# Row sums as a 65th column of the attention-value matmuls, and the copy of v in two halves

## The reference, cut to what matters

```python
xn = _layernorm(x, axis=-1)
s = _L0_attn_ref(xn, Wq, Wk, Wv, Wo)
g = _silu(_L0_ffn_ref(xn, rhs))
x = x + s * g
...
q = (x @ Wq.T).reshape(B, S, NHEAD, HEAD_DIM).transpose(0, 2, 1, 3)
k = (x @ Wk.T).reshape(B, S, NHEAD, HEAD_DIM).transpose(0, 2, 1, 3)
v = (x @ Wv.T).reshape(B, S, NHEAD, HEAD_DIM).transpose(0, 2, 1, 3)
...
# a query attends to the 128 keys up to and with its own
scores = jnp.einsum('bhcid,bhcjd->bhcij', qc, k2) / jnp.sqrt(D)
attn = jax.nn.softmax(jnp.where(valid, scores, -inf), axis=-1)
out = jnp.einsum('bhcij,bhcjd->bhcid', attn, v2)
return out.reshape(B, S, E) @ Wo.T
```

## Time and profile before

| | |
|---|---|
| median of 2 runs | 941.93 us (941.15 to 942.71) |
| the profiled execution | 942.05 us |
| its span, slowest core (core 7) | 940.5 us |
| spans of all cores | 928.4 to 940.5 us |
| mean granted TensorE clock of the cores | 0.967 to 0.975 |
| PE, DVE, ACT busy | 76%, 56%, 45% of the span |

### The profile page before, as it was taken

The page is one execution under the profiler, slowest core; times in us unless marked ns, Lnnn a source line. Parts: engine busy times, 40 slices in busy tenths (PEclk is TensorE's granted clock), DMA queues, the critical chain, the costliest instruction groups (busy, mean ns, idle before and its releaser), DMA issues.

```text
span 940.5 us, 15213 instructions; the slowest of 8 cores (928.4 to 940.5 us)
## 1 busy us (share of the span) xinstructions
PE 718.1 (76%) x5649; PEld 374.2 (40%) x5649; DVE 522.1 (56%) x984; ACT 424.5 (45%) x385; POOL 17.2 (2%) x36
## 2 busy tenths in 40 slices
PE   0000378888888888988888888888898899888874
PEld 0000234444444444444444444444444444444442
DVE  3235325666665566665665665655666665565632
ACT  0000145555555545555555555555554554554540
POOL 7000000000000000000000000000000000000000
PEclk9999999999999999999999999999999999999995
DMA  8991732444445434444343544444333444433421
GB/s 159 192 172 45 156 68 56 102 101 101 91 101 102 83 87 101 102 102 95 93 91 71 102 102 101 99 94 101 90 93 88 102 101 101 97 94 70 72 52 56
DMA packets 193048, 91.40 MB, mean 97 GB/s; under 512 B 179272, under 2 KB 179656, under 8 KB 192976
## 3 DMA queue, kind: packets, MB, share of 16 engines
q1 hardware_dynamic: 188368, 82.04, 38.7%
q0 software_dynamic: 4608, 8.39, 5.9%
HBM read 37.98 MB, written 16.78 MB: 58 GB/s over the span
## 4 chain that ended last, share of the span: by engine, by line
PE 52%; DMA 17%; ACT 15%; DVE 7%; issue 6%; SPq 2%; ACTq 0%; DVEq 0%
PE p_proj L461 37%; PE p_av L565 12%; DMA bfp<-bfp 11%; DMA scr<-rhst 6%; ACT bfp L402 4%; ACT bfp L428 3%; ACT bfp L406 3%; ACT bfp L387 3%; PE p_sc L478 1%; PE p_sc L483 1%; SPq L160 1%; DVE sm L292 1%; DVE scr L351 1%; ACT bfp L400 1%; DVE bfp L324 1%
## 5 line engine op out<-in xcount | busy, mean ns | idle before, releaser
L461 PE MATMUL p_proj<-wbf,bfp 128*128 128x512 bf16 x1536 | 367.2, 395 | 58.9 <-ACT bfp L406 31.6
L461 PEld LDWEIGHTS p_proj<-wbf,bfp 128*128 128x128 bf16 x1536 | 149.1, 101 | 241.0 <-issue 94.0
L461 PE MATMUL p_proj<-qrhs,bfp 128*128 128x512 bf16 x512 | 115.6, 379 | 43.6 <-ACT bfp L428 43.6
L565 PE MATMUL p_av<-wbf,bfp 128*128 128x512 bf16 x512 | 118.3, 385 | 4.9 <-DMA bfp<-bfp 4.9
L433 ACT ACTIVATE scr<-scr 128x1024 f32<-128x1024 f32 x32 | 33.8, 1056 | 173.9 <-DVE scr L342 173.9
L461 PEld LDWEIGHTS p_proj<-qrhs,bfp 128*128 128x128 bf16 x512 | 47.8, 97 | 111.5 <-issue 58.5
L381 ACT ACTIVATE bfp<-p_sc 128x2048 bf16<-128x2048 f32 x32 | 60.1, 1877 | 58.5 <-PE p_sc L483 56.3
L351 DVE TENSOR_TENSOR scr<-p_av,scr 128x1024 f32<-128x1024 f32 x32 | 39.2, 1225 | 76.8 <-PE p_av L565 76.8
L415 ACT ACTIVATE q32t<-scr,sm 128x1024 int32<-128x1024 f32 x32 | 36.8, 1148 | 93.3 <-DVE bfp L302 92.5
L565 PEld LDWEIGHTS p_av<-wbf,bfp 128*128 128x128 bf16 x512 | 50.7, 99 | 67.2 <-issue 8.5
L324 DVE TENSOR_TENSOR bfp<-bfp,mstd_s 128x2048 bf16<-128x2048 bf16 x60 | 71.0, 1222 | 4.7 <-ACT bfp L394 4.4
(11 more groups left out here) (58 smaller groups left out, 885.0 us busy)
## 6 DMA issues: line engine op xcount, KB each, us to landing
scr<-x SPq DMA_DIRECT2D x32, 512.0 KB, 4.8
y<-scr SPq DMA_DIRECT2D x32, 512.0 KB, 2.9
scr<-rhst SPq DMA_DIRECT2D x8, 512.0 KB
bfp<-bfp SPq DMA_TRANSPOSE x160, 3.2
wbf<-wqt POOLq DMA_DIRECT2D x8, 256.0 KB, 15.3
wbf<-wkt POOLq DMA_DIRECT2D x8, 256.0 KB, 25.7
wbf<-wvt POOLq DMA_DIRECT2D x8, 256.0 KB, 36.0
wbf<-wot POOLq DMA_DIRECT2D x8, 256.0 KB, 46.5
```

What stands on the lines that cost most here:

```text
L461: mms.append(lambda kc=kc, half=half: tensor.matmul(p_proj[:, half * 512:(half + 1) * 512], lhs_t[:, lhs_base + kc * 128:lhs_base + kc * 1 ...
L565: mms.append(lambda kc=kc, half=half, c=c: tensor.matmul(p_av[:, half * 512:(half + 1) * 512], bfp2[:, AOT[c % 2] + kc * 128:AOT[c % 2] + ...
```

## The change

The values of each head are stored with a stride of 65 instead of 64 columns; the 65th column of each head in both halves of `VS` is set to one once, at the start. A head's attention-value matmul reads 65 columns, so that the row sum comes out beside the 64 values, and the two matmuls against `onesc` are gone. The result goes to `p_sc`, 128 columns to a head, and no longer to `p_av`; VectorE's reciprocal and product read it there. The wait for `comb` of the previous chunk, which kept `AVS` from overwriting `p_av`, now stands ahead of the output projection.

ScalarE copies v out of `p_proj` in two instructions of 512 columns, with tags `vev0` and `vev`. The ffn projection waits for `vev0` ahead of its first matmul, which writes the first half, and for `vev` ahead of its second, which writes the other.

```diff
--- before.py
+++ after.py
@@ -33,11 +33,11 @@
 QB = [4096, 5120]
 QLT = [6144, 7168]
 KT = [8192, 9216]
-VS = [10240, 11264]
-QTF = 12288
-QTM = [13312, 15360]
-QROW, KROW = 17408, 18432
-BFP_COLS = 19456
+VS = [10240, 11280]
+QTF = 12352
+QTM = [13376, 15424]
+QROW, KROW = 17472, 18496
+BFP_COLS = 19520
 
 ERAW = 0
 EBF = 4096
@@ -226,7 +226,12 @@
             I(lambda: vector.memset(bfp[:, QTM[0]:QTM[0] + 2048], 0.0))
             I(lambda: vector.memset(bfp[:, QTM[1]:QTM[1] + 2048], 0.0))
             I(lambda: vector.memset(bfp[:, KT[1]:KT[1] + 1024], 0.0))
-            I(lambda: vector.memset(bfp[:, VS[1]:VS[1] + 1024], 0.0), "v", ("rings", 0))
+            SW(lambda: vector.memset(bfp[:, VS[1]:VS[1] + 1040], 0.0))
+            I(lambda: vector.memset(
+                bass.AP(bfp, VS[0] + 64, [[BFP_COLS, 128], [65, 16]]), 1.0))
+            I(lambda: vector.memset(
+                bass.AP(bfp, VS[1] + 64, [[BFP_COLS, 128], [65, 16]]), 1.0),
+              "v", ("rings", 0))
 
             def LN1(c):
                 Wv(vector, f"lx{c % 4}", 16 * (c // 4 + 1))
@@ -326,9 +331,11 @@
                 if 0 <= i < nchunk:
                     c = i
                     W(vector, "t", ("av", c))
-                    SW(lambda: vector.reciprocal(sm[:, RSUM:RSUM + 16], p_sc[:, 0:16]))
+                    SW(lambda: vector.reciprocal(
+                        sm[:, RSUM:RSUM + 16],
+                        bass.AP(p_sc, 64, [[2048, 128], [128, 16]])))
                     aov = bass.AP(bfp2, AO[c % 2], [[BFP2_COLS, 128], [64, 16], [1, 64]])
-                    pavv = bass.AP(p_av, 0, [[1024, 128], [64, 16], [1, 64]])
+                    pavv = bass.AP(p_sc, 0, [[2048, 128], [128, 16], [1, 64]])
                     rsv = bass.AP(sm, RSUM, [[64, 128], [1, 16], [0, 64]])
                     I(lambda a=aov, p=pavv, r=rsv: vector.tensor_tensor(a, p, r, ALU.mult),
                       "v", ("ao", c))
@@ -425,8 +432,15 @@
                 if 0 <= i + 1 < nchunk:
                     c = i + 1
                     W(scalar, "t", ("v", c))
-                    I(lambda c=c: scalar.copy(bfp[:, VS[c % 2]:VS[c % 2] + 1024],
-                                              p_proj[:, 0:1024]), "a", ("vev", c))
+                    I(lambda c=c: scalar.copy(
+                        bass.AP(bfp, VS[c % 2], [[BFP_COLS, 128], [65, 8], [1, 64]]),
+                        bass.AP(p_proj, 0, [[1024, 128], [64, 8], [1, 64]])),
+                      "a", ("vev0", c))
+                    I(lambda c=c: scalar.copy(
+                        bass.AP(bfp, VS[c % 2] + 8 * 65,
+                                [[BFP_COLS, 128], [65, 8], [1, 64]]),
+                        bass.AP(p_proj, 512, [[1024, 128], [64, 8], [1, 64]])),
+                      "a", ("vev", c))
                 if 0 <= i + 1 < nchunk:
                     c = i + 1
                     W(scalar, "v", ("ffne", c))
@@ -454,10 +468,12 @@
                                             start=True, stop=True)) for t in range(8)],
                 "t", ("rsb", 0))
 
-            def PROJ(c, name, lhs_t, lhs_base, rhs_t, rhs_base):
+            def PROJ(c, name, lhs_t, lhs_base, rhs_t, rhs_base, half1_wait=None):
                 mms = []
                 for kc in range(8):
                     for half in range(2):
+                        if kc == 0 and half == 1 and half1_wait is not None:
+                            mms.append(half1_wait)
                         mms.append(lambda kc=kc, half=half: tensor.matmul(
                             p_proj[:, half * 512:(half + 1) * 512],
                             lhs_t[:, lhs_base + kc * 128:lhs_base + kc * 128 + 128],
@@ -495,17 +511,11 @@
                     g, hh = divmod(h, 8)
                     e0 = EBF + g * 2048 + hh * 256
                     mms.append(lambda h=h, e0=e0: tensor.matmul(
-                        p_av[:, h * 64:h * 64 + 64], bfp2[:, e0:e0 + 128],
-                        bfp[:, vp_ + h * 64:vp_ + h * 64 + 64], start=True, stop=False))
+                        p_sc[:, h * 128:h * 128 + 65], bfp2[:, e0:e0 + 128],
+                        bfp[:, vp_ + h * 65:vp_ + h * 65 + 65], start=True, stop=False))
                     mms.append(lambda h=h, e0=e0: tensor.matmul(
-                        p_sc[:, h:h + 1], bfp2[:, e0:e0 + 128], onesc[:],
-                        start=True, stop=False))
-                    mms.append(lambda h=h, e0=e0: tensor.matmul(
-                        p_av[:, h * 64:h * 64 + 64], bfp2[:, e0 + 128:e0 + 256],
-                        bfp[:, vc_ + h * 64:vc_ + h * 64 + 64], start=False, stop=True))
-                    mms.append(lambda h=h, e0=e0: tensor.matmul(
-                        p_sc[:, h:h + 1], bfp2[:, e0 + 128:e0 + 256], onesc[:],
-                        start=False, stop=True))
+                        p_sc[:, h * 128:h * 128 + 65], bfp2[:, e0 + 128:e0 + 256],
+                        bfp[:, vc_ + h * 65:vc_ + h * 65 + 65], start=False, stop=True))
                 IMM(mms, "t", ("ava" if grp == 0 else "av", c))
 
             for i in range(-2, nchunk + 2):
@@ -538,8 +548,6 @@
                     c = i
                     W(tensor, "a", ("e1", c))
                     W(tensor, "v", ("e0m", c))
-                    if c >= 1:
-                        W(tensor, "v", ("comb", c - 1))
                     AVS(c, 0)
                     W(tensor, "v", ("e1m", c))
                     AVS(c, 1)
@@ -549,14 +557,17 @@
                     if c == 0:
                         Wv(tensor, "lwv", 128)
                     PROJ(c, "v", bfp, XNT[c % 2], wbf, 2 * 8192)
-                    W(tensor, "a", ("vev", c))
+                    W(tensor, "a", ("vev0", c))
                     Wv(tensor, f"trql{c % 2}", 16 * (c // 2 + 1))
                     if c == 0:
                         Wv(tensor, "trs", 128)
-                    PROJ(c, "ffn", bfp, QLT[c % 2], qrhs, 0)
+                    PROJ(c, "ffn", bfp, QLT[c % 2], qrhs, 0,
+                         half1_wait=lambda c=c: W(tensor, "a", ("vev", c)))
                 if 0 <= i < nchunk:
                     c = i
                     Wv(tensor, f"trao{c % 2}", 16 * (c // 2 + 1))
+                    if c >= 1:
+                        W(tensor, "v", ("comb", c - 1))
                     if c == 0:
                         Wv(tensor, "lwo", 128)
                     mms = []
```

## The result

The changed kernel takes 916.29 us in the median (11 runs), against 942.74 for the kernel before in the same comparison: a ratio of 0.9724, 95% interval 0.9691 to 0.9757. That is 26 us or 2.8% faster, where 932 (923 to 946) was forecast. The profiled execution took 916.13 us, with a span of 914.5. Executions in which a whole die ran at a lower clock are in the medians of all runs but in none of the ratios, so where the two differ, the ratio counts (two of the four runs of experiment 8 and five of the ten of experiment 5 were such, and their times are given without them).

The account below looks back on a forecast made before the run. The bound was a loop of about 24.5 us per chunk, 32 times, through projections, ScalarE copies and q's transposing DMA. 942.05 - 5.8 (split) - 3.2 (clock) - 0.6 (last chunk) = 932.4, given as 932 us, range 923 to 946.

Parts of the forecast that it names:

- The attention-value matmuls: TensorE, 64 matmuls to 32 per chunk: 0.82 us less work each, worth nothing on the path in 31 chunks.
- The moved wait for `comb`: Wait moved from ahead of the attention-value matmuls to ahead of the output projection: cost 0.
- the earlier VectorE and DMA steps: Reciprocal, product and output projection's transposing DMA start about 0.4 us earlier: worth nothing.
- The last chunk: Attention-value stage with no projection to cover it: 0.6 us saved of 2.7, bounds 0 and 1.3.
- The split: Copy of v in two halves, second ffn matmul earlier: 0.18 us per chunk, 5.8 us in all.
- the sentence of the bound itself: Copy of k (L406) sets the v projection's start and does not move, so halved attention-value matmuls gain nothing there.
- The clock: v projections at the slow clock: two fewer hits, 3.2 us; bounds four fewer (6.4) and two more (-3.2).
- the prediction's own sign: The prediction counts as wrong if, among other signs, the cold stretches change by more than four.
- More cold stretches from a wider gap: Rival: wider idle gap makes every v projection start at 1.2 GHz, 21 more paying 1.6 us: 970 us, chance 0.03.
- TensorE was not on the path: Rival claimed the opposite: TensorE on the path, so the attention-value saving of 26 us comes off: 906 us, chance 0.03.
- the strided copy: Rival: stride-65 writes slow ScalarE's half copies, up to 960 us; chance 0.12 of loss within 2%, 0.03 of more.
- The rule of the Trainium skill: TensorE idling between bursts of matmuls falls back to the slow clock and pays repeatedly; cited as speaking against the change.

Follow-up runs that it names:

- experiment 8: The change with ScalarE's copy of k moved ahead of its wait for q's transposing DMA and the copies of transposed q: 908.81 and 908.95 us.
- experiment 5: The change plus one small unread ScalarE copy just ahead of the copy of k, lengthening the quiet stretch about 0.5 us a chunk: ratio 1.0013.
- experiment 3: The kernel before with only the copy of v split in two halves, v stored as before: 933.75 us, ratio 0.9930.
- 4: The whole change with transposing-DMA sources kept at their old distance from a multiple of 2048 bytes: 925.54 us, ratio 0.9845.
- experiment 2: The kernel before with the attention-value part alone, one undivided copy of v, transposing-DMA sources at their old alignment: 943.7 us, ratio 1.0049.
- 1: The kernel before with only the change's addresses, everything behind v in the bf16 buffer 128 bytes further on: 930.65 us, ratio 0.9895.
- 6: The kernel before with only row-major q and k, sources of two transposing DMAs, moved by 128 bytes: 931.38 us, ratio 0.9909.
- experiment 7: The kernel before with the transposed q and its padded copies moved by 128 bytes, all sources keeping their alignment: 942.68 us, ratio 0.9993.
- 11: The change plus three more 512-column matmuls ahead of each output projection, outside the quiet stretch: 947.41 us, ratio 1.0066.
- 14: The kernel before with SyncE's load of x issued behind q's transposing DMA instead of ahead of it: 922.4 us, ratio 0.9803.
- 9: The change with the ffn projection's matmuls ordered half by half, waiting for the second copy of v between: 925.03 us, ratio 0.9820.
- 12: Half by half ffn and v projections, copy of k halved, all bf16 addresses 64 columns beyond the change's: 906.76 us, ratio 0.9633.

## Why the prediction was wrong

**The attention-value matmuls: right for the path, wrong for the whole.** They save 0.8 us a chunk on TensorE, the wait for the copy of k takes it up, and the second eight heads wait for the mask, all as foreseen. Alone they bring nothing (943.7 against 940.6, 5 us worse by the ratio, and 924.4 against 922.4 with the later load of x). But "on the path it is worth nothing" fails beside the split: from experiment 3 to 4 they bring 8 us, and the traces have a shorter q DMA (3.54 to 3.38 us in the mean, 5 us in 31 chunks) and 20 fewer cold stretches on eight cores (4 us a core). Why q's DMA gets shorter stays open.

**The moved wait for `comb`, the earlier VectorE and DMA steps: right**, no wait for any of them appears. **The last chunk**: 2.25 us (896.04 to 898.29) instead of 2.7, 0.45 saved where 0.6 was taken. At the low clock a pair of widths 64 and 1 had started every 80 ns, and a matmul of 65 columns starts every 55 ns, 0.8 us less in all; the second mask's wait took the rest.

**The split: right in kind, mis-sized.** The term was 0.18 us a chunk, 5.8 in all, and measured 0.26 and 8.1 (31 chunks). The price of a half was right (0.58 against 0.59), the overlap of two copies in a row was not: 0.11 us instead of the 0.05 read from L387 and L394. By itself the split brought 7 us; added to the attention-value part (experiment 2 to 4) it brought 19.

**Missing: the source address.** The failed step is the sentence of the bound itself, that L406 "does not move", with the DMA at a fixed 3.55. The sum has no term for that DMA, though the diff has a line for `QROW`: the constants were not looked at. The runs showed q's DMA at 3.26 us in the mean of all cores instead of 3.51, and experiments 1, 4, 6 and 7 that the source's address is worth 9 to 11 us.

**The clock: right in direction, far too small.** Two fewer cold stretches a core were taken, and the mean went from 9.25 to 2.5, some 6.75 x 1.6 = 11 us instead of 3.2. By the prediction's own sign, a change of more than four, this is a miss. It argued from the length of the chunk. Ten of the traces, over eight cores, with the loop from one v projection to the next (neither of them cold) and the quiet stretch in the median:

| kernel | loop, us | quiet stretch, us | q's DMA over 4.2 us | cold | cold in the other chunks |
|---|---|---|---|---|---|
| before | 24.36 | 3.61 | 9 | 74 | 65 |
| 7 | 24.29 | 3.51 | 14 | 65 | 52 |
| 11 | 24.29 | 3.09 | 40 | 46 | 12 |
| 2 | 24.12 | 3.37 | 34 | 61 | 30 |
| 1 | 24.11 | 3.31 | 7 | 33 | 27 |
| 5 | 24.09 | 3.64 | 21 | 67 | 46 |
| 3 | 24.06 | 3.54 | 34 | 49 | 18 |
| 14 | 23.99 | 3.13 | 9 | 18 | 11 |
| the change | 23.79 | 3.26 | 20 | 20 | 6 |
| 9 | 23.67 | 3.28 | 50 | 37 | 7 |

Loops of one length have very different counts (12 and 52 in the last column at 24.29). In all traces but that of experiment 8, 283 of the 359 chunks with a slow q DMA are cold, and 354 of the other 3857. So a long quiet stretch goes with the fall of the clock, and a slow q DMA makes one; a shorter one, as the moved source gives, goes with fewer. The stretch does not decide alone (experiment 3 has 18 in the last column, before 65, with nearly the same stretch); what else does stays open, the length of the loop included.

**The account** of 26 us, by edit and by the ratios: the split alone 7, the attention-value part on top of it 8, the addresses on top of both 11. In another order the numbers differ: addresses alone 10, attention-value part alone -5, the split on top of that 19. The addresses are thus worth about the same in any company; it is the split and the attention-value part that depend on each other. By place, in the traces' means over the cores: cold stretches 11 us, the copy of v to the last ffn matmul 8, q's DMA 8 (0.25 us in 31 chunks), together 27. The cores' spans are 27 us shorter in the mean.

**The rivals.** More cold stretches from a wider gap did not come; TensorE was not on the path; the strided copy costs nothing extra (1.01 us in experiment 2). The rule of the Trainium skill named in the prediction ("TensorE: Matmul & The Clock Gate", on HAM oscillation) pointed the wrong way for the total, since the change has fewer cold stretches although TensorE idles longer ahead of the v projection (39.2 us in all instead of 31.6). Chunk by chunk the trace agrees with it: a v projection is cold mostly where the quiet stretch ahead of it is long, 4.7 us in the median against 3.2.

## What to carry to other kernels

Before counting what an edit removes, read its constants: where a buffer lies can be worth more than the instructions, and a kernel that moves only addresses costs one run to try. When a part alone measures as nothing and two together as more than their sum, look for something that all of them share, here the clock's cold stretches and two DMAs in one queue, and take it away before comparing parts. Measure a part beside the others too, and not only alone: the split was worth 7 us in one company and 19 in another. A DMA on the path should not be issued right behind a large load that nobody needs yet.

## What the hardware showed that was not expected

A transposing DMA of 128 x 1024 bf16 from SBUF to SBUF lands in 3.0 us at the least when its source starts at a multiple of 2048 bytes in the partition or 256 past one, and in 2.7 to 2.8 us when it starts 128 bytes past, for all five transposes of the loop (experiments 1 and 12); the address of q's destination made no difference (experiment 7). The Trainium skill ("DMA: Bandwidth & Descriptors", section "How a descriptor splits into AXI transactions") says that a descriptor which doesn't start on a boundary of 256 bytes has its first transaction start at the boundary below, and that the bytes fetched ahead of its start still cost; by it the moved sources should have been no faster. Here they were faster, and the measurement decides; other distances were not tried.

Two copies of 512 columns from PSUM by ScalarE, 0.59 us each, start 0.48 us apart, so that splitting a copy of 1.01 us costs only 0.06. The granted clock over a run can depend on tenths of a microsecond in a loop's quiet stretch: 0.5 us more per chunk, put there, cost 27 us where 16 were added (experiment 5, 67 cold stretches instead of 20).
